# Chunks of an edge list laid out in pairs: one accumulator add per two chunks, a PSUM home for each kind of group, and a copy made in two halves

## The reference, cut to what matters

```python
xc = x[row]
xn = x[col]
h = relu(xc @ W1[:d] + xn @ W1[d:] + b1)
mask = sigmoid(h @ W2 + b2)[:, 0]
seg_sum = segment_sum(mask, row, num_segments=n)
w = mask / (seg_sum[row] + 1e-09)
agg = segment_sum(w[:, None] * xn, row, num_segments=n)
deg = segment_sum(ones_like(mask), row, num_segments=n)
out_emb = where((deg > 0)[:, None], 0.5 * x + 0.5 * agg, x)
return relu(out_emb @ Wl + bl)
```

## Time and profile before

| what | value |
|---|---|
| median of 3 runs | 4378.5 us (4376.01 to 4381.13) |
| profiled execution, its own time | 4369.24 us |
| its span, first to last instruction | 4367.5 us |
| mean granted TensorE clock | 0.879 |
| busy in the span | PE 3569.9 us (82%), PEld 2439.5 (56%), DVE 3158.9 (72%), ACT 2150.9 (49%), POOL 1555.6 (36%) |

### The profile page before, as it was taken

How to read it: one execution, slowest core, us unless ns; L and a number is a source line. 1 busy time by engine, 2 the same in 40 slices (tenths; PEclk the granted TensorE clock), 3 DMA queues, 4 the chain that set the end, 5 groups by cost and what they waited for, 6 DMA issues and landing times. The chain is left out here.

```text
span 4367.5 us, 95747 instructions
## 1 busy us (share of the span) xinstructions
PE 3569.9 (82%) x20539; PEld 2439.5 (56%) x20540; DVE 3158.9 (72%) x12757; ACT 2150.9 (49%) x6722; POOL 1555.6 (36%) x1256
## 2 busy tenths in 40 slices
PE   4868882698888999986997996888888888888883
PEld 2367771333333444433444444777777778777783
DVE  8999987698888888873003005888888888888886
ACT  0078884266677888872003003444444444444444
POOL 0068874000000000001002002777777777777770
PEclk8855555799999999997998998999999999999996
DMA  2011113001111222224874882444444444444451
GB/s 47 1 10 15 15 17 81 10 34 51 68 68 77 95 93 103 94 86 187 303 276 165 304 297 85 144 137 141 138 138 142 136 141 138 137 138 140 141 134 40
DMA packets 276115, 498.31 MB, mean 114 GB/s; under 512 B 92068, under 2 KB 192571, under 8 KB 275883
## 3 DMA queue, kind: packets, MB, share of 16 engines
q1 hardware_dynamic: 209550, 347.01, 23.8%
q0 software_dynamic: 66336, 149.10, 12.4%
HBM read 391.18 MB, written 104.79 MB: 114 GB/s over the span
## 5 line engine op out<-in xcount | busy, mean ns | idle before, releaser
L1684 POOL DMA_INDIRECT xs<-edge_table,ea_row_stage x1088 | 1104.7, 1015 | 448.9 <-issue 432.7
L1868 PE MATMUL ea_psa<-xs,slot_dst 128*128 128x129 f32 x3264 | 458.5, 285 | 231.3 <-DVE agg_t L1782 231.2
L1868 PEld LDWEIGHTS ea_psa<-xs,slot_dst 128*128 128x128 f32 x3264 | 416.2, 195 | 264.3 <-DVE agg_t L1782 257.5
L1235 PE MATMUL a_agg_ps<-a_adj_ring,parts 128*128 128x512 f16 (+1 forms) x2548 | 523.6, 369 | 46.0 <-DMA a_adj_ring<-adjacency 45.9
L1902 ACT ACTIVATE slot_dst<-ea_onehot,ea_mask 128x128 f32<-128x128 f16 x1632 | 535.7, 399 | 13.2
L1782 DVE TENSOR_TENSOR agg_t<-agg_t,ea_psa 128x129 f32 x1632 | 460.5, 282 | 109.9 <-PE ea_psa L1868 97.5
L1034 PE MATMUL ab_agg_ps<-ab_adj_stage,parts 128*128 128x512 f16 x1911 | 529.6, 388 | 0.0
L1896 ACT ACTIVATE ea_mask<-ea_dot,b 128x4 f32<-128x4 f32 x408 | 121.3, 297 | 771.7 <-DVE slot_src L1807 771.7
L449 ACT ACTIVATE dst_step<-iota,dst_low_bias 128x128 f16<-128x128 f16 x1188 | 358.1, 401 | 216.0 <-PEq L474 213.0
L429 POOL DMA_INDIRECT records<-both_parts,record_row x98 | 348.5, 3556 | 314.8 <-ACT both_parts L455 291.8
L1375 POOL TENSOR_TENSOR parts<-xs,parts 128x896 f16<-128x896 f32 x7 | 13.2, 1881 | 1224.7 <-ACT parts L1369 1224.7
(11 more groups left out here) (379 smaller groups left out, 6463.6 us busy)
## 6 DMA issues: line engine op xcount, KB each, us to landing
a_adj_ring<-adjacency SPq DMA_DIRECT2D x182, 896.0 KB, 4.6
ea_low_rows<-low_rows SPq DMA_DIRECT2D x411, 128.0 KB
adjacency<-ab_adj_stage SPq DMA_DIRECT2D x91, 512.0 KB, 2.6
adjacency<-ab_adj_stage SPq DMA_DIRECT2D x91, 384.0 KB, 2.3
ea_near_rows<-near_rows SPq DMA_DIRECT2D x137, 128.0 KB
xs<-edge_table,ea_row_stage POOLq DMA_INDIRECT x1088
edge_table<-vx SPq DMA_DIRECT2D x12, 512.0 KB, 2.9
ea_row_stage<-row_columns SPq DMA_DIRECT2D x272, 2.0 KB
```

The source lines that it names most:

```text
L1235: ins = nc.tensor.matmul(ps[:, h, 0:width], lhs(r, t), ring[:, g % SLOTS, k * DB:k * DB + width], start=t == 0 and r == 0, stop=t == NT - ...
L1684: nc.gpsimd.indirect_dma_start(got[:, h, g, k, 0:ROW], None, m.table, bass.IndirectOffsetOnAxis(ap=row_s[:, h, g, k:k + 1], axis=0)).then_ ...
L1868: ins = nc.tensor.matmul(psa[:, home, k, 0:AW], hot_m[:, g, k, :], what, start=True, stop=True)
```

## The change

1. **Chunks in pairs.** A tile gets `2 * ceil(edges / 256)` chunks, so chunks 2q and 2q + 1 always belong to one tile. The inputs' counts per tile (3363 to 4220 edges) give 1614 chunks in place of 1586. The arrays grow with that (`SC` 1616 to 1660).
2. **One add per pair.** TensorE sums two chunks in the same PSUM place (`start=k % 2 == 0, stop=k % 2 == 1`), and VectorE adds once per pair: 6 adds in a step in place of 12.
3. **A home for each kind.** `psa` is `[P, 3, 2, 256]`: the sums of kind `g` only wait for the adds of the same kind one step before.
4. **The copy in two halves.** ScalarE copies the near rows of chunks 0 and 1, then of 2 and 3, and VectorE waits for the first half ahead of score 0 and for the second ahead of score 2.
5. **The plan counts what is filled.** The number of groups with edges (`filled`) is computed on VectorE from the number of chunks, `(1614 + 3) >> 2` = 404 here, and near groups are at most `filled * 21845 >> 16` = 134. Worked out from the edge lists, there are 142 near groups, so 134 are taken, and `m.pairs` is `(404 + 3 - 134) >> 2` = 68.

```diff
-SC = 1616
+SC = 1660
...
-NEAR = GROUPS // 3
+assert GROUPS * 21845 < 1 << 24
...
-            ch(nc.vector.tensor_scalar(chf[:, :], carry[0:NT, :], float(P - 1), None, ALU.add))
+            ch(nc.vector.tensor_scalar(chf[:, :], carry[0:NT, :], float(2 * P - 1), None, ALU.add))
             ch(nc.vector.tensor_copy(chi[:, :], chf[:, :]))
-            ch(nc.vector.tensor_scalar(chi[:, :], chi[:, :], 7, None, ALU.arith_shift_right))
+            ch(nc.vector.tensor_scalar(chi[:, :], chi[:, :], 8, None, ALU.arith_shift_right))
             ch(nc.vector.tensor_copy(chf[:, :], chi[:, :]))
-            ch(nc.vector.tensor_scalar(chf[:, :], chf[:, :], 1.0, None, ALU.max))
+            ch(nc.vector.tensor_scalar(chf[:, :], chf[:, :], 1.0, 2.0, ALU.max, ALU.mult))
...
             ch(nc.vector.tensor_reduce(narrow[:, :], line[:, 2, 0:SC].rearrange("o (g k) -> o g k", k=4), AX.X, ALU.min))
+            ch(nc.vector.tensor_scalar(filled[:, :], m.first_chunk[0:1, NT:NT + 1], 3.0, None, ALU.add))
+            ch(nc.vector.tensor_copy(filled_i[:, :], filled[:, :]))
+            ch(nc.vector.tensor_scalar(filled_i[:, :], filled_i[:, :], 2, None, ALU.arith_shift_right))
+            ch(nc.vector.tensor_copy(filled[:, :], filled_i[:, :]))
+            ch(nc.vector.tensor_scalar(room_i[:, :], filled_i[:, :], 21845, None, ALU.mult))
+            ch(nc.vector.tensor_scalar(room_i[:, :], room_i[:, :], 16, None, ALU.arith_shift_right))
+            ch(nc.vector.tensor_copy(room[:, :], room_i[:, :]))
+            ch(nc.vector.scalar_tensor_tensor(narrow[:, :], ordinal[:, :], filled[:, 0:1], narrow[:, :], ALU.is_le, ALU.mult))
...
-        psa = ctx.enter_context(nc.psum_tensor("ea_psa", [P, 2, G, 256], F32))
+        psa = ctx.enter_context(nc.psum_tensor("ea_psa", [P, 3, 2, 256], F32))
...
-                if seen >= 2 or g or k:
-                    dve.wait_ge(s_add, t * 12 + (g * G + k + 4))
+                if seen >= 2 or g or q:
+                    dve.wait_ge(s_add, t * 6 + (g * 2 + q + 10))
                 dst = m.acc[:, bass.ds(tile_at(tile), 1), :].rearrange("p o w -> p (o w)")
-                ins = nc.vector.tensor_tensor(dst, dst, psa[:, home, k, 0:AW], ALU.add)
+                ins = nc.vector.tensor_tensor(dst, dst, psa[:, g, q, 0:AW], ALU.add)
...
                     else:
                         adds[0]()
-                        dve.wait_ge(s_near_x, t + 1)
+                        dve.wait_ge(s_near_x, 2 * t + 1)
...
                     for k in range(G):
+                        if g == NEARBY and k == 2:
+                            dve.wait_ge(s_near_x, 2 * t + 2)
...
-                        if k in (0, 2):
-                            adds[1 + k // 2]()
+                        if k == 1:
+                            adds[1]()
                     if g == 0:
                         dve.wait_ge(s_low[1 - h], i * 64 + (64 + 64 * h))
                     transposed(g, 1 - h, t)
-                    adds[3]()
...
-                if seen >= 2 or g == NEARBY:
-                    pe.wait_ge(s_add, t * 12 + 4 * g)
+                if seen >= 2:
+                    pe.wait_ge(s_add, t * 6 + (2 * g + 6))
                 for k in range(G):
                     what = near_x[:, k, 0:AW] if g == NEARBY else got[:, h, g, k, D:D + AW]
-                    ins = nc.tensor.matmul(psa[:, home, k, 0:AW], hot_m[:, g, k, :], what, start=True, stop=True)
+                    ins = nc.tensor.matmul(psa[:, g, k // 2, 0:AW], hot_m[:, g, k, :], what, start=k % 2 == 0, stop=k % 2 == 1)
...
-                        nc.scalar.activation(near_x[:, :, 0:D], psv[:, :, 1, :], ACT.Copy).then_inc(s_near_x, 1)
+                        for a in (0, 2):
+                            nc.scalar.activation(near_x[:, a:a + 2, 0:D], psv[:, a:a + 2, 1, :], ACT.Copy).then_inc(s_near_x, 1)
```

More of the change, by code:

```diff
@@ L27 @@
 CC = BLOCKS * K
-ROWS = 2 * SC + P
+ROWS = 2 * SCP + P
 DB = 512
@@ L43 @@
 GW = TG * P
-assert SC >= (N_EDGES // P) + NT and (P * K + NT * (2 * LANES - 2)) // LANES <= P and CC + K <= SCP and 2 * SCP <= ROWS
+assert SC >= 2 * (N_EDGES // (2 * P) + NT) and SC <= SCP and (P * K + NT * (2 * LANES - 2)) // LANES <= P and CC + K <= SCP and SC + 4 <= SCP
 class Chain:
@@ L337, in _ @@
             pe.wait_ge(s_chunks, 1)
-            nc.tensor.matmul(psr[:, 0:NT], chb[:, :], m.before[0:NT, 0:NT], start=True, stop=True)
+            nc.tensor.matmul(psr[:, 0:NT + 1], chb[:, :], m.before[0:NT, 0:NT + 1], start=True, stop=True)
             nc.tensor.matmul(psr[0:NT, 64:65], m.before[0:NT, 0:NT], chf[:, :], start=True, stop=True).then_inc(s_first, 1)
@@ L765, in plan_edges @@
         half, trips = sb("half", [1, 1]), sb("trips", [1, 1], I32)
+        filled, filled_i = sb("filled", [1, 1]), sb("filled_int", [1, 1], I32)
+        room, room_i = sb("room", [1, 1]), sb("room_int", [1, 1], I32)
         column = sb("column", [P, NB4])
@@ L817, in _ @@
             nc.vector.tensor_scalar(to_far[:, :], to_far[:, :], -1.0, None, ALU.add).then_inc(s_slots, 1)
-            ch(nc.vector.tensor_scalar(half[:, :], taken[:, GROUPS - 1:GROUPS], -1.0, float(GROUPS + 3), ALU.mult, ALU.add))
+            ch(nc.vector.scalar_tensor_tensor(half[:, :], filled[:, :], 3.0, taken[:, GROUPS - 1:GROUPS], ALU.add, ALU.subtract))
             ch(nc.vector.tensor_copy(trips[:, :], half[:, :]))
@@ L980, in load @@
                                                             skip_runtime_bounds_check_because="the tables hold counts")[1][0:n]
-        COUNTS = (1 << 20) - 1
+        COUNTS = (1 << 21) - 1
         assert NQ * SC <= COUNTS
@@ L1772, in transposed, with add @@
                 ins.then_inc(s_hot_t[g], 1)
-            def add(t, g, k, tile, home, seen):
-                if k == 0:
+            def add(t, g, q, tile, seen):
+                if q == 0:
                     dve.wait_ge(s_agg[g], t)
-                if seen >= 2 or g or k:
-                    dve.wait_ge(s_add, t * 12 + (g * G + k + 4))
+                if seen >= 2 or g or q:
+                    dve.wait_ge(s_add, t * 6 + (g * 2 + q + 10))
                 dst = m.acc[:, bass.ds(tile_at(tile), 1), :].rearrange("p o w -> p (o w)")
-                ins = nc.vector.tensor_tensor(dst, dst, psa[:, home, k, 0:AW], ALU.add)
+                ins = nc.vector.tensor_tensor(dst, dst, psa[:, g, q, 0:AW], ALU.add)
                 ins.then_inc(s_add, 1)
@@ L1792, in step @@
                 for g in KINDS:
-                    adds = [lambda k=k: add(t, g, k, v[4 * g + k], (h + 1 + g) % 2, seen) for k in range(G)] if seen >= 1 else [lambda: None] * G
+                    adds = [lambda q=q: add(t, g, q, v[4 * g + 2 * q], seen) for q in (0, 1)] if seen >= 1 else [lambda: None] * 2
                     dve.wait_ge(s_u[g], t + 1)
@@ L1821, in after @@
                 for g in KINDS:
-                    for k in range(G):
-                        add(end * 2, g, k, v[4 * g + k], (1 + g) % 2, 2)
-                dve.wait_ge(s_add, end * 24 + 16)
+                    for q in (0, 1):
+                        add(end * 2, g, q, v[4 * g + 2 * q], 2)
+                dve.wait_ge(s_add, end * 12 + 16)
                 dve.sem_inc(s_seen_dve, 1)
@@ L1846, in lookups @@
                     if seen >= 1:
-                        pe.wait_ge(s_near_x, t)
+                        pe.wait_ge(s_near_x, 2 * t)
                     for k in range(G):
@@ L1878, in step @@
                     if seen >= 1:
-                        sums(t, g, 1 - h, (h + 1 + g) % 2, seen)
+                        sums(t, g, 1 - h, seen)
             def after(end):
                 for g in KINDS:
-                    sums(end * 2, g, 1, (1 + g) % 2, 2)
+                    sums(end * 2, g, 1, 2)
             turns(pe, step, after=after)
```

16 lines of the change are left out of this document (8 added, 8 removed).

## The result

The changed kernel takes 4250.14 us in the median of 4 runs (4245.02 to 4253.77), beside 4377.35 us (4376.01 to 4381.13, 4 runs) for the kernel before: a ratio of 0.9707, 95% interval 0.969 to 0.9724, 127 us less. Forecast were 4279 us, 100 less than before, and the measured median lies at the very edge of the range of 4250 to 4325. The sign, the stage and the engine that becomes the bound came out as written. The gain was larger than forecast: 124 us between the two profiled executions (4369.24 and 4245.02) in place of 100.

What follows compares the result with a forecast made beforehand. The VectorE loop with its ScalarE detour was taken as the bound, GpSimd as the next. Gathers 100 us and stage end 9 less, first steps 3 more, 6 taken off: 100 us saved, 4279 us; range 4250 to 4325.

Steps and rivals of the forecast that it cites:

- What bounds the kernel before: Edge stage: VectorE's whole work plus the detour through ScalarE sets the 11.34 us step; GpSimd is 0.8 us away.
- GpSimd becomes the bound: Edge stage, the forecast case: eight gathers need 10.56 us against VectorE's 10.00; 4279 us (4262 to 4298), chance 0.62.
- Is 10.56 itself steady?: GpSimd's gathers beside VectorE's f16 one-hots: their 0.51 us excess grows by 7%, 0.04, making the step 10.60 us.
- The third rival: Gathers slow down only beside work now elsewhere: 10.05 us a step, 175 us less, 4203 us; chance 0.06.
- VectorE's loop: Edge stage step: 11.34 less 1.00 (adds), 0.14 (near copy), 0.20 (PSUM homes) comes to 10.00 us.
- kind 1's last add: One of six adds removed on VectorE; lies in the shadow of the wait for ScalarE and frees nothing.
- The end of the stage: From last gather to last add: 20.9 us before, 12 after, so 9 us less.
- the 9 us held back for the first steps and for unseen waits: Taken off the saving: 3 us for first steps that VectorE and buffers still pace, 6 us for waits no row shows.
- the gather term: Edge stage, 1087 gather distances, each shortened from 1.417 us to 10.60/8: 100 us less.
- The plan stage: Eight more small VectorE instructions, under 2 us together, hidden behind PE's 64 products: 0.
- TensorE's accumulation: Summing pairs in PSUM: PE's instructions are the same in number and size, so 0.
- the number of steps: Edge stage: 136 steps and 1088 gathers as before, since the 28 more chunks fill groups that were empty.

Runs made afterwards that it cites:

- run 3: Six gathers a step in place of eight (fourth chunk's rows zeros) in the kernel before: 4364.04 us, ratio 0.9981.
- run 2: Six gathers a step in place of eight (fourth chunk's rows zeros) in the changed kernel: 4128.64 us, ratio 0.9434 to the kernel before.
- Run 4: Changed kernel with each kind's f16 one-hots behind its group's scores, not in one block at the step's start: 4257.05 us, ratio 0.9736.
- run 1: The changed kernel itself again, no edit, on chip 13 beside the kernel before: 4248.87 us against 4372.14, ratio 0.9711.

## Why the prediction was right in kind and short in size

**What bounds the kernel before: right as far as shown.** GpSimd was close behind and not the bound: in run 3 six gathers in place of eight save 8 us. That VectorE's loop with its detour over ScalarE set the step is argued from the timeline and the waits, not shown by a run of its own.

**GpSimd becomes the bound: right**, shown by run 2 (120 us less when it is relieved) and by the 0.307 us of idle time ahead of each gather.

**The step that failed** is "Is 10.56 itself steady?", the term "That makes 10.60". It let the excess of a gather over 951 ns grow by 7%, because GpSimd no longer idles and the f16 work stands in a shorter step. Measured are 8 x (0.997 + 0.305) = 10.42 us by the same formula, 10.43 by the distances: the excess fell from 0.064 to 0.045 us. 10.60 - 10.43 = 0.17 us in 136 steps are 23 us, nearly all of the 24 us by which the profiled execution (4245.02) lies under the forecast for it (4269). The third rival, *GpSimd gets faster too*, had the right direction and too large a size (10.05 us a step): the f16 work stayed, as was held against it, and yet the gathers got shorter.

The mistake was to take the lengthening of a gather as a share of the time in which VectorE works. The trace shows that it hangs at least in part on the moment. These are two neighbouring gathers of the kernel after and VectorE's instructions at their starts (start us, us):

```profile
3499.52 0.97 DVE L1781 TENSOR_SCALAR xs<-ea_near_rows,row_ids 128x512 f32<-128x512 f16 x2
...
3500.16 1.15 POOL L1694 DMA_INDIRECT xs<-edge_table,ea_row_stage  x1 [0.31 <-issue]
...
3501.60 0.69 DVE L1807 TENSOR_TENSOR slot_src<-ea_psz,xs 128x512 f32<-128x512 f32 x1
3501.62 0.96 POOL L1694 DMA_INDIRECT xs<-edge_table,ea_row_stage  x1 [0.30 <-issue]
```

The first starts inside a f16 one-hot and takes 1.15 us; the second starts with the f32 `z` and takes 0.96. Counted over the gathers in the trace: where a f16 one-hot of VectorE ran 0.2 us after the gather's start, the mean was 1.097 us before the change (412 gathers) and 1.082 after (279); all others had 0.965 and 0.968. The number of one-hots is the same; the number of gathers that meet one at that moment fell by a third, and with it the time over 0.957 us of these gathers, by 23 us. After the change VectorE waits for the gathers in most steps (118 times), so it runs more in step with them, which would explain it.

Run 4 puts the one-hots elsewhere, and there the count carries less. In run 1, 296 gathers meet one (mean 1.070 us) and 792 don't (0.972); in run 4 it is 392 (1.053) and 696 (0.982). Of the 10 us by which the gathers got longer, the first kind has some 4, the others some 6. So where the one-hots stand matters, by the one shift made; that the meeting at this moment is the cause isn't settled. After the change, too, 71 gathers took over 1.03 us with no one-hot at that moment.

The Trainium skill (SBUF — State Buffer, section "SBUF: two separate sides") has GpSimd kept from writing descriptors until a VectorE instruction in a two-port mode is over. The trace agrees in that gathers beside f16 one-hots are longer, by 0.1 to 0.2 us; no row tells in which mode these run. The forecast had drawn from the page that a denser VectorE would disturb more, and the measurement went the other way.

**VectorE's loop: 10.00 forecast, 9.61 measured** (run 2, with TensorE near its own limit). It decided nothing, since GpSimd is longer than either. The median steps of the kernel before and of run 2, worked out from the starts in both traces, tell the terms. `z` of kind 0 to `z` of kind 1 went from 2.67 to 2.24 us, two adds. `z` of kind 1 to its last score went from 1.85 to 1.63, one add; the detour from there to the start of the near copy stayed at 1.88, so kind 1's last add, which stands beside it, freed nothing, as forecast. From the start of the near copy to the first near score it went from 0.61 to 0.39, so the copy gave 0.22 us and not 0.14 (a half copy takes 0.364 us, forecast 0.43). On to the next `z` it went from 3.87 to 3.48, two adds. So five adds count, 1.00 us, as forecast. The rest of 11.34 - 9.61 = 1.73 us, some 0.5, shows only in the means, so in the steps longer than the median: fewer late results of TensorE and less waiting for the next numbers, where the forecast had 0.2. What each edit is worth by itself on a chip like the document's isn't shown: all runs that undo one edit fell on the other kind.

**The end of the stage: 12 us forecast.** From the last gather to the last add it is 18.4 us, by these rows of DVE and 20.9 before:

```profile
4141.89 0.29 DVE L1792 TENSOR_TENSOR agg_t<-agg_t,ea_psa 128x129 f32 x1 [1.00 <-PE ea_psa L1879]
...
4146.74 0.49 DVE L1778 TENSOR_SCALAR ea_onehot_t<-ea_low_rows,row_ids 128x512 f32<-128x512 f16 x1 [3.52 <-DMA ea_near_rows<-near_rows]
4147.15 0.68 DVE L1807 TENSOR_TENSOR slot_src<-ea_psz,xs 128x512 f32<-128x512 f32 x1
...
4156.29 0.72 DVE L1792 TENSOR_TENSOR agg_t<-agg_t,ea_psa 128x129 f32 x2 [1.28 <-PE ea_psa L1879]
```

In the last step an add of kind 0 waits 1.00 us for the sums, a load of one-hot keys comes 3.52 us late, a wait that the forecast didn't have, and the last adds wait 1.28 us: 5.8 of the 6.4 us over the 12. The forecast let the last `z` start when its rows land, 3.1 us after the last gather's start; it starts 8.6 us after it (4147.15 against 4138.6), behind VectorE's work for kind 0 and these waits. Against that, the 9 us held back for the first steps and for unseen waits among the gathers weren't needed beside the 10.43 us a step, and the first gather starts 1.1 us later than before. These nearly cancel (9 - 6.4 - 1.1 = 1.5), so the 24 us are the gather term's. The whole: 123.2 us between first and last gather, 2.5 at the end, less 1.1 at the start, 124.6, and the spans differ by 124.2.

**The plan stage, TensorE's accumulation, the number of steps: right**, at nothing each that shows. Of the signs that were named, the counts, the idle time before gathers and the wait ahead of `z` came; the mean gather (0.997 us) and the half copies (0.364) didn't.

## What to carry to other kernels

When two loops are close, price both: the shorter path is worth only the distance to the next bound (here 0.9 us of the 1.7 us taken off VectorE's path), and taking work off the next engine in the kernel before and after (8 us and 120 us) shows whether it paces. An engine that becomes the bound must be priced in the phase that it will then have against its neighbours, with both ends in the range; a mean taken while it was being held back isn't its mean. Time a change on more than one chip, and the version to compare with on each: here the same pair of kernels gave 0.971 on two sets of runs and 0.992 on a third, and eight runs of its variants on slow chips have no changed kernel beside them.

## What the hardware showed that was not expected

- Some chips run this stage 300 us slower, the same kernel, every execution: 4679 to 4714 us on chips 3, 4, 7 and 12, 4372 on chip 13. In the changed kernel's trace on chip 3, TensorE's instructions inside a group start 0.7 us or more apart hundreds of times where 0.11 is usual (270 us in 1320). What it waits for is not in the trace, and the cause stays open.
- On such a chip six useless adds a step made the changed kernel 31 us faster (4608.21 against 4639.35).
- A gather of 128 rows took 0.957 us (median), 1.08 in the mean where a f16 one-hot of VectorE ran 0.2 us after its start, and 0.968 where none did.
- Loading a step's numbers on TensorE's queue took 1.10 us, and TensorE stood still for 1.4 us around it once the waits that hid it were gone.
- ScalarE's copy of 256 columns from PSUM took 0.364 us, that of 512 columns 0.582 us in the mean, and an activation of 4 columns 0.30: half the columns cost much more than half the time.
